# A decoder layer's feed-forward stage on one core: VectorE's list reordered, and two small computations moved to ScalarE

## The chip, the cores and the metric

The kernel runs on one core of a Trainium2 chip. The metric is device time in microseconds (us) from start to end of one execution. A core has five engines that each work through a list of their own, in order: TensorE (PE in the profile, its weight loads PEld), VectorE (DVE), ScalarE (ACT), GpSimd (POOL) and SyncE (SP, which here only starts DMAs). They are kept in step by semaphores alone: an instruction waits until a semaphore has reached a value, and what stands behind it in its engine's list waits too.

## The reference, cut to what matters

The program computes one decoder layer for 2048 tokens (4 sequences of 512) of width 512: attention with a sliding window, a layer in which each token goes through one of four experts, and a quantized gated feed-forward. Only the last is touched by the change. For a token row x (normalized without weights):

```
def activation_quant(x):                       # 8 bits, one scale per token
    s = 127 / clip(max(abs(x)), 1e-5)
    return clip(round(x * s), -128, 127) / s
def weight_quant(w):                           # -1, 0 or 1, one scale per matrix
    s = 1 / clip(mean(abs(w)), 1e-5)
    return clip(round(w * s), -1, 1) / s
h = silu(bit_linear(x, w_gate)) * bit_linear(x, w_up)     # 512 -> 2048
h = ln_weight * h * rsqrt(mean(h * h) + 1e-6)
y = bit_linear(h, w_down)                                 # 2048 -> 512
x = x + y
```

So the down product is one of small integers, multiplied at the end by a factor per token: the largest of the token's |h * ln_weight * rsqrt(...)| / 127 times the mean of |w_down|. In the kernel this factor is `y_scale`.

## The kernel before, in words

The feed-forward (`ffn_phase`, from L1580) goes over 16 tiles of 128 tokens, one token per partition. The 2048 h values of a token are made in FC = 4 chunks of 512 columns, called h value 0 to 3 here (the change calls them first to fourth). The work of a tile is spread over several rounds of the loops; every engine has one loop `for t in range(TILES)`, and in round t it does this:

- TensorE (`tensor_program`, L1881; `gate_up`, L1649): for each chunk c four matmuls for the gate and four for the up product of tile t, 512 columns each, and after each chunk a quarter of the down product of an earlier tile (LATE_DOWN = 2: two tiles back). The products go to two pairs of PSUM tiles in turn, so `gate_up(t, c)` waits until h value c - 2 has been formed (counted over the tiles too: `gate_up(t, 0)` waits for h value 2 of tile t - 1, `gate_up(t, 1)` for h value 3 of it, L1654). In the profile the gate tiles are `e_xT_ps` (even c) and `e_z_ps` (odd c), the up tiles `up_ps` and `e_aT_ps`.
- ScalarE (`scalar_program`, L1728): `gate_of(t, c)` (L1746) is the Silu of the gate product; `squares` (L1754) sums the squares of one half of h, 1024 columns; `pack` (L1739) turns the quantized half into bf16. The list of a round is: squares(t-1, 1), gate 0, normalize x of tile t+2, gate 1, turn-over of x's transpose, gate 2, pack(t-1, 0), pack(t-1, 1), gate 3, squares(t, 0).
- VectorE (`vector_program`, L1779): `hidden(t, c)` (L1784) forms h value c out of the up product and the gate. `top_of(t-1, n)` (L1800) is the largest of a half of the weighted h of the tile before, `sum_squares` (L1805 and L1807) forms its mean square plus epsilon, `scale_h` (L1813 to L1822) forms the factors, among them `y_scale` (L1819), `quantize_h` (L1831) multiplies and rounds both halves, and `y_of` (L1836) adds a finished down product to x. The rest is the normalization and quantization of x for tiles t+2 and t+3 (`front...`).
- GpSimd (`gpsimd_program`, L1681): h_rms as the power -0.5 of h_var (L1691), the weighting `weighted(t, c)` of each h value by `ln_w` into `xg_own` (L1695), two small operations for x, and the indirect DMAs that store a finished tile and gather a new one. In round t its list is: h_rms of t-1, weighted 0, 1, 2, rstd for x, weighted 3, gu_scale, store, gather.
- SyncE: the DMA transposes of the packed h (all tiles but the last, which TensorE transposes).

Each list is written out by hand; nothing plans it. Before the loop the experts' stage also forms the means of the three quantized weights, `w_mean`, and their reciprocals `w_scale` (L1462 and L1464), which ScalarE waits for before it quantizes the weights (L1380).

Of the kernel before, what the change touches and what calls it, by code (L numbers as in the profile page):

```python
# [54 lines left out]
CODE, CODE_ZERO = ROUND + 0x6600, 1536.0  # L55
XQ_STEPS, HQ_STEPS = 3, 5
LATE_DOWN = 2
# [1163 lines left out]
def expert_phase(nc, ctx, scratch, io, x1, x2, sh, front):  # L1221
# [7 lines left out]
    def sb(name, shape, dt=F32):  # L1229
        return ctx.enter_context(nc.sbuf_tensor(name, shape, dt))  # L1230
# [16 lines left out]
    abs_sum, abs_row, w_scale = sh["abs_sum"], sb("abs_row", [P, 3]), sb("w_scale", [P, 3])  # L1247
    plus_round = sb("plus_round", [P, 1])
    e_ones = sb("e_ones", [P, P])
    bn_st, bn_mv = sb("e_bn_st", [P, 2, 6]), sb("e_bn_mv", [P, 2, 2])  # L1250
# [118 lines left out]
    def scalar_program(act):  # L1369
# [6 lines left out]
        def shift(n):  # L1376
            c = stage_of(n)
            w = n // WCHUNKS
            act.wait_ge(w_loaded[c], n // STAGES * 16 + 16)
            act.wait_ge(scales_ready, 1)  # L1380
            nc.scalar.activation(w_stage[:, c, :], w_stage[:, c, :], ACT.Identity, scale=w_scale[:, w:w + 1], bias=plus_round[:])\
                .then_inc(w_shifted, 1)
# [27 lines left out]
    def vector_program(dve):  # L1410
# [51 lines left out]
        nc.vector.tensor_scalar(w_mean[:], sum_ps[:], 1.0 / (D * F), Q_EPS, ALU.mult, ALU.max).then_inc(mean_ready, 1)  # L1462
        dve.wait_ge(mean_ready, 1)
        nc.vector.reciprocal(w_scale[:], w_mean[:]).then_inc(scales_ready, 1)  # L1464
        dve.wait_ge(scales_ready, 1)

# [113 lines left out]
def ffn_phase(nc, ctx, io, x2, y, sh, front):  # L1580
# [31 lines left out]
    hw_max = sb("hw_max", [P, 2, 2])  # L1612
    h_ss, h_var, h_rms = sb("h_ss", [P, 1]), sb("h_var", [P, 1]), sb("h_rms", [P, 1])
    h_top, h_max, h_inv, h_mul = sb("h_top", [P, 1]), sb("h_max", [P, 1]), sb("h_inv", [P, 1]), sb("h_mul", [P, 1])
    y_scale = sb("y_scale", [P, LATE_DOWN + 2])

# [12 lines left out]
    hw_last_ready = sem("hw_last_ready")  # L1629
    ss_ready, h_var_ready, rms_ready = sem("ss_ready"), sem("h_var_ready"), sem("rms_ready")  # L1630
    hq_step, hq_ready = sem("hq_step"), sem("hq_ready")
# [96 lines left out]
    def scalar_program(act):  # L1728
# [12 lines left out]
        def gate_of(t, c):  # L1741
            act.wait_ge(gate_summed, t * FC + c + 1)
            act.wait_ge(gu_ready, t + 1)
            if c >= 2 or inside(t - 1):
                act.wait_ge(h_ready, t * FC + c - 1)
            nc.scalar.activation(gate[:, c % 2, :], gate_ps[c % 2][:], ACT.Silu, scale=gu_scale[:, t % 2, 0:1])\  # L1746
                .then_inc(gate_ready, 1)

        def squares(t, n):
            i = t % 2  # L1750
            act.wait_ge(h_ready, t * FC + 2 * n + 2)
            if n or inside(t - 1):
                act.wait_ge(sq_ready, t * HALVES + n)
            nc.scalar.activation(sq_junk[:], flat(h, i)[:, n * HALF:n * HALF + HALF], ACT.Square,  # L1754
                                 accum_out=h_sq[:, i, n:n + 1]).then_inc(sq_ready, 1)

        for t in range(TILES):
# [14 lines left out]
            if t == TILES - 1:  # L1772
                pack(t - 1, 1)
            squares(t, 0)
        squares(TILES - 1, 1)
        for g in range(FC):
            hqT_of(TILES - 1, g)

    def vector_program(dve):  # L1779
# [23 lines left out]
        def sum_squares(t):  # L1803
            dve.wait_ge(sq_ready, (t + 1) * HALVES)
            nc.vector.tensor_reduce(h_ss[:], h_sq[:, t % 2, :], AX.X, ALU.add).then_inc(ss_ready, 1)  # L1805
            dve.wait_ge(ss_ready, t + 1)
            nc.vector.tensor_scalar(h_var[:], h_ss[:], 1.0 / F, RMS_EPS, ALU.mult, ALU.add).then_inc(h_var_ready, 1)  # L1807

        def scale_h(t):
            i = t % 2  # L1810
            at = t * HQ_STEPS
            dve.wait_ge(hw_max_ready, (t + 1) * HALVES)
            nc.vector.tensor_reduce(h_top[:], hw_max[:, i, :], AX.X, ALU.max).then_inc(hq_step, 1)  # L1813
            dve.wait_ge(hq_step, at + 1)
            dve.wait_ge(rms_ready, t + 1)
            nc.vector.tensor_scalar(h_max[:], h_top[:], h_rms[:], Q_EPS, ALU.mult, ALU.max).then_inc(hq_step, 1)
            dve.wait_ge(hq_step, at + 2)
            nc.vector.reciprocal(h_inv[:], h_max[:]).then_inc(hq_step, 1)
            nc.vector.tensor_scalar(y_scale[:, t % (LATE_DOWN + 2):t % (LATE_DOWN + 2) + 1], h_max[:], w_mean[:, 2:3], 1.0 / QMAX, ALU.mult, ALU.mult)\  # L1819
                .then_inc(hq_step, 1)  # L1820
            dve.wait_ge(hq_step, at + 4)
            nc.vector.tensor_scalar(h_mul[:], h_inv[:], h_rms[:], QMAX, ALU.mult, ALU.mult).then_inc(hq_step, 1)  # L1822
# [11 lines left out]
        def y_of(t):  # L1834
            dve.wait_ge(y_summed, t + 1)
            nc.vector.scalar_tensor_tensor(xt[t], sums_of(t), y_scale[:, t % (LATE_DOWN + 2):t % (LATE_DOWN + 2) + 1], xt[t],  # L1836
                                           ALU.mult, ALU.add).then_inc(y_ready, 1)

        for t in range(TILES):
# [4 lines left out]
            if inside(t - LATE_DOWN - 1):  # L1844
                y_of(t - LATE_DOWN - 1)
            if inside(t - 1):
                top_of(t - 1, 1)
            hidden(t, 0)
# [3 lines left out]
            if inside(t - 1):  # L1852
                sum_squares(t - 1)
            if inside(t + 2):
                front.top_of_x(dve, t + 2)
# [3 lines left out]
            if inside(t - 1):  # L1859
                scale_h(t - 1)  # L1860
                quantize_h(t - 1)
            hidden(t, 2)
            if inside(t + 2):
# [162 lines left out]
```

## Time and profile before

| | |
|---|---|
| median of 3 runs | 789.06 us (788.45 to 791.21) |
| the profiled execution | 788.65 us, of which the trace's span is 786.6 us |
| TensorE busy | 734.1 us, 93% |
| VectorE busy | 592.7 us, 75% |
| ScalarE busy | 473.0 us, 60% |
| GpSimd busy | 331.8 us, 42% |
| mean granted TensorE clock | 0.989 |

The feed-forward's loop takes the part of the span from about 591 us to its end. In it the busy shares differ from the table: in the 40 slices of the profile, TensorE and VectorE both show 9 tenths or nearly there, ScalarE 6 to 7. Start times are counted from the first instruction; "busy" excludes semaphore waits; the name in a row's brackets is what an idle engine was released by. Successive instructions of one engine can overlap by some hundredths of a microsecond, so for the length of a list the distances from start to start count.

### The profile page before, as it was taken

The numbers are of one execution on the slowest core, as the hardware profiler recorded it, in microseconds if no ns is written. First come the engines' busy times: TensorE is split into PE (matmuls) and PEld (weight loads), VectorE is DVE, ScalarE is ACT, GpSimd is POOL, SyncE is SP. The second block draws the span as 40 slices with busy tenths as digits, with TensorE's granted clock in tenths as the row PEclk, the third lists the DMA queues.
The fourth block names the chain that finished last, engine by engine and source line by source line (L and its number), as shares of the span: only waits on it lengthen the run. The fifth ranks groups of instructions, "written<-read, shape, count | busy, mean of one in ns | idle before, by whom it ended". The sixth has DMA issues, their size and how long they took to land.

```text
span 786.6 us, 14189 instructions
## 1 busy us (share of the span) xinstructions
PE 734.1 (93%) x5167; PEld 509.8 (65%) x5184; DVE 592.7 (75%) x1099; ACT 473.0 (60%) x1028; POOL 331.8 (42%) x329
## 2 busy tenths in 40 slices
PE   5988999999999999999987989999998999999993
PEld 4765777777777776777764678888874444444441
DVE  6886866886667866766666547888888999999992
ACT  4565666766676665766666314444456777667761
POOL 2011205213242134254554444445546577778661
PEclk9999999999999999999999999999999999999998
DMA  9300012304030321314301366555341133334241
GB/s 311 119 1 27 28 47 89 105 31 162 29 108 28 108 93 70 108 38 152 129 34 55 54 216 261 186 200 196 118 134 30 41 95 80 98 91 107 70 92 40
DMA packets 55474, 78.33 MB, mean 100 GB/s; under 512 B 36335, under 2 KB 38383, under 8 KB 53680
## 3 DMA queue, kind: packets, MB, share of 16 engines
q1 hardware_dynamic: 46336, 51.99, 20.8%
q0 software_dynamic: 8784, 24.93, 9.7%
q8 instruction: 43, 0.70, 0.4%
q10 hardware_dynamic: 288, 0.52, 0.2%
q14 instruction: 23, 0.19, 0.1%
HBM read 56.92 MB, written 17.59 MB: 95 GB/s over the span
## 4 chain that ended last, share of the span: by engine, by line
PE 61%; DVE 21%; issue 7%; ACT 5%; POOL 3%; DMA 1%; another core or an unknown queue 0%; SPq 0%; ACTq 0%; POOLq 0%; DVEq 0%
PE side_ps L889 17%; PE pT_ps L976 9%; PE e_z_ps L1528 7%; PE y_ps L1528 7%; PE s_ps L948 5%; PE pv_ps L998 5%; DVE h L1784 4%; DVE hw_max L1800 4%; DVE hq_big L1831 3%; ACT hq L1739 2%; DVE neg_max L724 2%; PE s_ps L956 2%; PE pT_ps L889 1%; DVE probs L745 1%; ACT probs L548 1%
## 5 line engine op out<-in xcount | busy, mean ns | idle before, releaser
L548 ACT ACTIVATE probs<-s_ps,neg_max 128x512 f32<-128x512 f32 (+2 forms) x256 | 152.3, 610 | 18.6 <-DVE neg_max L724 17.1
L724 DVE TENSOR_REDUCE neg_max<-s_ps 128x2 f32<-128x1024 f32 (+2 forms) x128 | 124.5, 1014 | 36.2 <-PE s_ps L956 35.1
L976 PE MATMUL pT_ps<-ident,probs 128*128 128x128 f32 x832 | 115.7, 281 | 8.7 <-DVE probs L745 8.0
L560 ACT ACTIVATE probs<-pT_ps 128x512 f32<-128x512 f32 x96 | 57.4, 598 | 97.0 <-PE pT_ps L976 96.2
L976 PEld LDWEIGHTS pT_ps<-ident,probs 128*128 128x128 f32 x832 | 94.3, 144 | 23.9 <-DVE probs L745 10.6
L745 DVE COPY probs<-pT_ps 128x512 f32<-128x512 f32 x112 | 76.7, 685 | 38.9 <-PE pT_ps L976 35.9
L1695 POOL TENSOR_TENSOR xg_own<-h,ln_w_sb 128x512 f32<-128x512 f32 x63 | 82.8, 1324 | 33.2 <-DVE h L1784 33.1
L889 PE MATMUL side_ps<-w_hi 128*128 128x512 f32 x172 | 71.0, 413 | 0.0
L412 POOL TENSOR_TENSOR aT_hi<-norm,one_col 128x512 fp32r<-128x512 f32 x15 | 15.6, 1042 | 124.6 <-DVE norm L736 86.3
L889 PE MATMUL side_ps<-w_hi,w_lo 128*128 128x512 f32 x172 | 67.4, 392 | 0.0
L889 PE MATMUL side_ps<-w_lo,w_hi 128*128 128x512 f32 x172 | 67.0, 390 | 0.0
L1906 PE MATMUL y_ps<-w_tern,hqT 128*128 128x512 bf16 x210 | 54.5, 379 | 0.7
L998 PE MATMUL pv_ps<-probs,v_sb 128*32 128x256 f32 (+1 forms) x896 | 52.4, 368 | 1.9 <-DVE probs L745 0.9
L404 POOL TENSOR_TENSOR norm<-rinv,one_col 128x512 f32<-128x512 f32 x16 | 16.7, 1041 | 86.8 <-DVE rinv L731 86.8
L548 ACT ACTIVATION_READ_ACCUMULATOR probs<-s_ps,neg_max 128x1 f32 x256 | 52.9, 207 | 0.0
L1739 ACT ACTIVATE hq<-hq_big,minus_offset 128x1024 bf16<-128x1024 f16 x30 | 33.0, 1142 | 30.4 <-DVE hq_big L1831 30.4
L1657 PE MATMUL e_xT_ps<-w_tern,xqT_home 128*128 128x512 bf16 x126 | 32.7, 380 | 7.1 <-DVE h L1784 6.2
L1800 DVE TENSOR_REDUCE hw_max<-xg_own 128x1 f32<-128x1024 f32 x32 | 38.7, 1209 | 0.3
L998 PEld LDWEIGHTS pv_ps<-probs,v_sb 128*32 128x32 f32 x896 | 25.0, 109 | 19.6 <-issue 6.7
L889 PEld LDWEIGHTS side_ps<-w_hi,w_lo 128*128 128x128 f32 x172 | 32.3, 188 | 7.4
L1906 PEld LDWEIGHTS y_ps<-w_tern,hqT 128*128 128x128 bf16 x224 | 21.4, 98 | 23.3
L889 PEld LDWEIGHTS side_ps<-w_hi 128*128 128x128 f32 x172 | 32.4, 188 | 5.8 <-DVE k_lo L648 0.5
(290 smaller groups left out, 1782.8 us busy)
## 6 DMA issues: line engine op xcount, KB each, us to landing
w_piece<-w_ffn SPq DMA_DIRECT2D x24, 512.0 KB
w_stage<-w_ffn SPq DMA_DIRECT2D x12, 1024.0 KB
xres<-x POOLq DMA_DIRECT2D x4, 1024.0 KB, 6.4
xn<-x SPq DMA_DIRECT2D x3, 1024.0 KB
x<-xres POOLq DMA_DIRECT2D x3, 1024.0 KB, 4.8
xn<-c SPq DMA_DIRECT2D x2, 1024.0 KB, 5.0
v_next<-c SPq DMA_DIRECT2D x2, 1024.0 KB, 7.3
xn<-x SPq DMA_DIRECT2D x4, 256.0 KB, 3.7
```

Source lines behind the costliest of these rows:

```text
L548: nc.scalar.activation(weights[qt][:, h, at:at + width(qt)], s_ps[:, h, 0:width(qt)], ACT.Exp, bias=neg_max[:, qt % 2, h:h + 1], accum_out ...
L560: nc.scalar.activation(out, turned_p, ACT.Identity).then_inc(slot_copied[0], 1)
L724: nc.vector.tensor_reduce(neg_max[:, qt % 2, 2 * s:2 * s + 2], s_ps[:, 2 * s:2 * s + 2, 0:width(qt)], AX.X, ALU.max, negate=True).then_inc ...
L745: nc.vector.tensor_copy(weights[qt][:, :, a:z], pT_ps[:, 1, :].rearrange("p (h n) -> p h n", h=GH))\
L889: last = nc.tensor.matmul(out, lt, r, start=(first and n == 0), stop=(final and n == len(terms) - 1))
L976: last = nc.tensor.transpose(pT_ps[:, k % 2, h * P:h * P + P], weights[qt][:, h, a:z], ident[:])
L998: last = nc.tensor.matmul(pv_ps[HD * h:HD * h + HD, to], v_sb[:, slot, f:f + HD], p, start=first, stop=final, tile_position=(0, HD * h))
L1528: last = nc.tensor.matmul(out, lt[:, k, :], r[:, at, :], start=(n == 0), stop=(n == 3 * DK - 1))
L1695: nc.gpsimd.tensor_tensor(hw[:, t % 2, c, :], h[:, t % 2, c, :], ln_w[:, c * CHK:c * CHK + CHK], ALU.mult)\
L1739: nc.scalar.activation(hq[:, cols], hq_code[:, cols], ACT.Identity, bias=minus_offset[:]).then_inc(hq_packed, 1)
L1800: nc.vector.tensor_reduce(hw_max[:, i, n:n + 1], flat(hw, i)[:, n * HALF:n * HALF + HALF], AX.X, ALU.max, apply_absolute_value=True).then_ ...
L1906: last = nc.tensor.matmul(sums_of(t), hqT[:, t % 2, k, :], down_w[:, k, :], start=(k == 0), stop=(k == FK - 1))
```

## The change

VectorE's list in round t, before and after (what concerns x stays in place):

| before | after |
|---|---|
| mean of x, top 0, y_of | mean of x, top 0, y_of |
| **top 1**, h value 0, sum_squares | h value 0, sum_squares, **top 1** |
| top of x, h value 1, scale x, scale_h | top of x, h value 1, scale x, scale_h |
| **quantize_h**, h value 2 | h value 2, **quantize_h** |
| quantize x, statistics of x, h value 3 | quantize x, statistics of x, h value 3 |

sum_squares shrinks from two dependent instructions to one, since ScalarE now scales the values by 2048 ** -0.5 inside the Square activation. scale_h loses the forming of `y_scale`; ScalarE forms it with one activation on 128x1 values, at the end of round t for tile t - 1 (and for the last tile at the end), from `down_scale`, which VectorE forms once in the experts' stage.

```diff
-XQ_STEPS, HQ_STEPS = 3, 5
+XQ_STEPS, HQ_STEPS = 3, 4
...
+    down_scale = sh["down_scale"] = sb("down_scale", [P, 1])
...
-            act.wait_ge(scales_ready, 1)
+            act.wait_ge(scales_ready, 2)
...
+        nc.vector.tensor_scalar(down_scale[:], w_mean[:, 2:3], 1.0 / QMAX, None, ALU.mult).then_inc(scales_ready, 1)
         nc.vector.reciprocal(w_scale[:], w_mean[:]).then_inc(scales_ready, 1)
-        dve.wait_ge(scales_ready, 1)
+        dve.wait_ge(scales_ready, 2)
...
+        def y_scale_of(t):
+            n = t % (LATE_DOWN + 2)
+            act.wait_ge(hq_step, t * HQ_STEPS + 2)
+            if t >= LATE_DOWN + 2:
+                act.wait_ge(y_ready, t - LATE_DOWN - 1)
+            nc.scalar.activation(y_scale[:, n:n + 1], h_max[:], ACT.Identity, scale=down_scale[:]).then_inc(y_scale_ready, 1)
+
         def squares(t, n):
...
-            nc.scalar.activation(sq_junk[:], flat(h, i)[:, n * HALF:n * HALF + HALF], ACT.Square,
+            nc.scalar.activation(sq_junk[:], flat(h, i)[:, n * HALF:n * HALF + HALF], ACT.Square, scale=F ** -0.5,
...
             squares(t, 0)
+            if inside(t - 1):
+                y_scale_of(t - 1)
         squares(TILES - 1, 1)
+        y_scale_of(TILES - 1)
...
-            nc.vector.tensor_reduce(h_ss[:], h_sq[:, t % 2, :], AX.X, ALU.add).then_inc(ss_ready, 1)
-            dve.wait_ge(ss_ready, t + 1)
-            nc.vector.tensor_scalar(h_var[:], h_ss[:], 1.0 / F, RMS_EPS, ALU.mult, ALU.add).then_inc(h_var_ready, 1)
+            nc.vector.tensor_scalar(h_var[:], h_sq[:, t % 2, 0:1], h_sq[:, t % 2, 1:2], RMS_EPS, ALU.add, ALU.add)\
+                .then_inc(h_var_ready, 1)
...
+            if inside(t - 1):
+                dve.wait_ge(y_scale_ready, t)
             nc.vector.tensor_scalar(h_max[:], h_top[:], h_rms[:], Q_EPS, ALU.mult, ALU.max).then_inc(hq_step, 1)
...
-            nc.vector.tensor_scalar(y_scale[:, t % (LATE_DOWN + 2):t % (LATE_DOWN + 2) + 1], h_max[:], w_mean[:, 2:3], 1.0 / QMAX, ALU.mult, ALU.mult)\
-                .then_inc(hq_step, 1)
-            dve.wait_ge(hq_step, at + 4)
+            dve.wait_ge(hq_step, at + 3)
...
             dve.wait_ge(y_summed, t + 1)
+            dve.wait_ge(y_scale_ready, t + 1)
...
-            if inside(t - 1):
-                top_of(t - 1, 1)
             hidden(t, 0)
...
                 sum_squares(t - 1)
+                top_of(t - 1, 1)
...
                 scale_h(t - 1)
+            hidden(t, 2)
+            if inside(t - 1):
                 quantize_h(t - 1)
-            hidden(t, 2)
```

## Rows read from the trace of the kernel before

**Rows 1.** Windows, one round: us, busy us PE, PEld, DVE, ACT, POOL, clock, DMA.
```profile
653.34:664.58 11.24, 10.87 (x53) 4.76 (x53) 10.85 (x24) 8.07 (x13) 8.49 (x11) 1.00 0.34 93
```

**Rows 2.** Chain that ended last, same round: start us, us, what.
```profile
649.21 1.31 DVE hq_big L1831
...
653.34 0.75 DVE h L1784
```

**Rows 3.** Timeline of VectorE: start us, us, engine, line, operation, out<-in [idle before].
```profile
642.12 0.75 DVE L1784 SCALAR_TENSOR_TENSOR h<-e_aT_ps,gu_scale,f_gate 128x512 f32<-128x512 f32 x1
...
644.69 1.21 DVE L1800 TENSOR_REDUCE hw_max<-xg_own 128x1 f32<-128x1024 f32 x1
645.82 0.74 DVE L1784 SCALAR_TENSOR_TENSOR h<-up_ps,gu_scale,f_gate 128x512 f32<-128x512 f32 x1
646.48 0.14 DVE L1805 TENSOR_REDUCE h_ss<-h_sq 128x1 f32<-128x2 f32 x1
646.65 0.15 DVE L1807 TENSOR_SCALAR h_var<-h_ss 128x1 f32<-128x1 f32 x1
...
648.65 0.17 DVE L1818 RECIPROCAL h_inv<-h_max 128x1 f32<-128x1 f32 x1
648.73 0.20 DVE L1819 TENSOR_SCALAR y_scale<-h_max,w_mean 128x1 f32<-128x1 f32 x1
648.96 0.21 DVE L1822 TENSOR_SCALAR h_mul<-h_inv,h_rms 128x1 f32<-128x1 f32 x1
649.21 1.96 DVE L1831 TENSOR_SCALAR hq_big<-xg_own,h_mul 128x1024 f32<-128x1024 f32 x2
651.09 0.74 DVE L1784 SCALAR_TENSOR_TENSOR h<-up_ps,gu_scale,f_gate 128x512 f32<-128x512 f32 x1
...
653.08 0.15 DVE L1181 TENSOR_SCALAR f_var_eps<-f_bn_mv 128x1 f32<-128x1 f32 x1
```

**Rows 4.** Timeline of ScalarE, same round.
```profile
650.54 2.19 ACT L1739 ACTIVATE hq<-hq_big,minus_offset 128x1024 bf16<-128x1024 f16 x2 [2.17 <-DVE hq_big L1831]
652.64 0.67 ACT L1746 ACTIVATE f_gate<-e_z_ps,gu_scale 128x512 f32<-128x512 f32 x1
...
654.15 0.19 ACT L1754 ACTIVATION_READ_ACCUMULATOR sq_junk<-h 128x1 f32 x1
654.44 1.06 ACT L1754 ACTIVATE sq_junk<-h 128x1024 bf16<-128x1024 f32 x1
...
655.49 0.67 ACT L1746 ACTIVATE f_gate<-e_xT_ps,gu_scale 128x512 f32<-128x512 f32 x1
```

**Rows 5.** Groups of ScalarE by form: the smallest activation.
```profile
L525 ACT ACTIVATE k_hi<-side_ps,bk_sb 128x4 fp32r<-128x4 f32 x15 | 3.7, 245 | 0.0
```

**Rows 6.** Timeline of TensorE: the product that waits for h value 0.
```profile
646.61 1.04 PE L1657 MATMUL e_xT_ps<-w_tern,xqT_home 128*128 128x512 bf16 x4 [0.29 <-DVE h L1784]
```

**Rows 7.** Timeline of GpSimd, same round.
```profile
647.44 2.51 POOL L1695 TENSOR_TENSOR xg_own<-h,ln_w_sb 128x512 f32<-128x512 f32 x2
...
651.91 1.45 POOL L1695 TENSOR_TENSOR xg_own<-h,ln_w_sb 128x512 f32<-128x512 f32 x1 [1.96 <-DVE h L1784]
```

**Rows 8.** Timelines of the last tile but one: GpSimd, VectorE, ScalarE.
```profile
749.61 1.72 POOL L1695 TENSOR_TENSOR xg_own<-h,ln_w_sb 128x512 f32<-128x512 f32 x1
...
750.11 1.76 DVE L1831 TENSOR_SCALAR hq_big<-xg_own,h_mul 128x1024 f32<-128x1024 f32 x1
...
751.91 1.15 ACT L1739 ACTIVATE hq<-hq_big,minus_offset 128x1024 bf16<-128x1024 f16 x1 [0.53 <-DVE hq_big L1831]
...
753.67 0.75 DVE L1784 SCALAR_TENSOR_TENSOR h<-e_aT_ps,gu_scale,f_gate 128x512 f32<-128x512 f32 x1 [1.13 <-ACT f_gate L1746]
```

**Rows 9.** Timelines, the first and the last regular rounds: ScalarE, then VectorE.
```profile
600.10 0.67 ACT L1746 ACTIVATE f_gate<-e_xT_ps,gu_scale 128x512 f32<-128x512 f32 x1
...
609.00 0.75 DVE L1784 SCALAR_TENSOR_TENSOR h<-e_aT_ps,gu_scale,f_gate 128x512 f32<-128x512 f32 x1
...
743.17 0.75 DVE L1784 SCALAR_TENSOR_TENSOR h<-e_aT_ps,gu_scale,f_gate 128x512 f32<-128x512 f32 x1 [1.11 <-ACT f_gate L1746]
```

More of the change, by code:

```diff
@@ L1612, in ffn_phase @@
     hw_max = sb("hw_max", [P, 2, 2])
-    h_ss, h_var, h_rms = sb("h_ss", [P, 1]), sb("h_var", [P, 1]), sb("h_rms", [P, 1])
+    h_var, h_rms = sb("h_var", [P, 1]), sb("h_rms", [P, 1])
     h_top, h_max, h_inv, h_mul = sb("h_top", [P, 1]), sb("h_max", [P, 1]), sb("h_inv", [P, 1]), sb("h_mul", [P, 1])
-    y_scale = sb("y_scale", [P, LATE_DOWN + 2])
+    y_scale, down_scale = sb("y_scale", [P, LATE_DOWN + 2]), sh["down_scale"]
     hq_code = hq_big[:].bitcast(F16)[:, 0:2 * F:2]
@@ L1629, in ffn_phase @@
     hw_last_ready = sem("hw_last_ready")
-    ss_ready, h_var_ready, rms_ready = sem("ss_ready"), sem("h_var_ready"), sem("rms_ready")
+    h_var_ready, rms_ready, y_scale_ready = sem("h_var_ready"), sem("rms_ready"), sem("y_scale_ready")
     hq_step, hq_ready = sem("hq_step"), sem("hq_ready")
```

## The prediction

> **What bounds the kernel now.** I read the page's busy shares first, then the windows of a round, the chain of waits, and the timelines of the engines side by side. The loop runs in rounds of 11.22 us. In one, TensorE is busy 10.87 and VectorE 10.85 us [rows 1], so both look full, and TensorE once a round stands idle for 0.29 us until VectorE has formed h value 0 [rows 6]. That is the view in which moving h values forward looks right. The chain of waits shows something else: the round is closed by a ring that goes through ScalarE as well. It leads from the first half of quantize_h to h value 3 [rows 2] in 653.34 - 649.21 = 4.13 us, and what lies between is ScalarE's: pack 0 starts as the first half is written (650.54), pack 1 follows, and gate 3, which stands behind both in ScalarE's list, starts at 652.64 and ends at 653.31 [rows 4], 0.03 us ahead of h value 3. VectorE had started its last small instruction before that at 653.08 [rows 3]: it was ready a little before the gate, by some 0.2 us. So VectorE's list is the bound from h value 3 round to quantize_h, and ScalarE's from quantize_h to h value 3. A round is the sum of three legs:
>
> - h value 3 (642.12) to h value 0 (645.82): 3.70 us, VectorE's list [rows 3].
> - h value 0 to quantize_h (649.21): 3.39 us, VectorE's list [rows 3].
> - quantize_h to h value 3: 4.13 us, through ScalarE [rows 2, 4].
>
> Beside the first leg runs a second path, which is not yet late: gate 3, squares(t, 0), squares(t, 1), gate 0. Gate 0 starts 655.49 - 652.64 = 2.85 us after gate 3 and ends at 656.16 [rows 4]. Gate 3 starts 0.70 us ahead of h value 3, and h value 0 can start 0.03 us behind gate 0's end, so this path makes the leg at least -0.70 + 2.85 + 0.70 = 2.85 us. It has 0.85 us to spare.
>
> **The change part by part.**
>
> *Leg 1, h value 3 to h value 0.* top 1 leaves it: 645.82 - 644.69 = 1.13 us [rows 3]. VectorE's list would then need 3.70 - 1.13 = 2.57 us, but gate 0 is not there before 2.85. New on ScalarE, between squares(t, 0) and squares(t, 1), is the activation for y_scale. Before, squares(t, 1) started at 654.44, 0.10 after the accumulator read of squares(t, 0) had ended at 654.34 [rows 4]; that gap, about 0.1, takes part of the new instruction. Its price: no 128x1 activation is in the trace; the nearest is 128x4 at 0.245 us [rows 5], upper bound 0.67 - 0.10 = 0.57 (a 512-wide gate less the overlap with what follows it), lower bound 0, if it fits in the gap. I take 0.245 less about 0.1 of overlap with the next, less the part in the gap: 0.1. Its waits are met long before (h_max was written in the middle of the round, the y_of that frees the buffer two rounds ago). Leg 1: 2.95 us. So 0.75 is gained of the 1.13 taken out, and VectorE then idles some 0.4 us ahead of h value 0.
>
> By the Trainium skill (ScalarE: Activation LUTs, what an ACTIVATE costs), an activation with immediates takes 186 ns plus 0.833 ns per element, each per-partition pointer about 93 ns more, and successive ones overlap by about 93 ns. By that estimate the new one takes 0.19 us of the list; no run here shows it yet, and leg 1 would be 2.95 with it too.
>
> *Leg 2, h value 0 to quantize_h.* Added: top 1, 1.13, and h value 2, 646.48 - 645.82 = 0.66 [rows 3]. Gone: the sum of the squares, 646.65 - 646.48 = 0.17; y_scale, which stood between h_inv and h_mul: h_mul started 0.31 behind h_inv (648.65 to 648.96) and must now wait for h_inv itself, 0.17 and about 0.04 of semaphore (649.21 - 648.96 - 0.21), so 0.10 less; and quantize_h no longer starts right behind the h_mul that it needs: h value 2 needs nothing of it and can start 0.13 behind h_mul (0.21 less the 0.08 by which successive instructions overlap, as 645.82 + 0.74 and 646.48 show) where quantize_h needed 0.25, so 0.12 less. Leg 2: 3.39 + 1.13 + 0.66 - 0.17 - 0.10 - 0.12 = 4.79 us. No other wait is late in it: TensorE starts the product for h value 2 behind h value 0 [rows 6] and gate 2 is ready about 2.7 us after h value 0, h value 2 comes 4.1 after it. h_var is ready earlier in the list than before, and h_rms with it.
>
> *Leg 3, quantize_h to h value 3.* VectorE's list loses h value 2 here, 0.66, but the leg goes by ScalarE, so this gives nothing: VectorE waits longer for gate 3. What counts is when the two halves are written, and there GpSimd enters. The first half takes 1.31 us [rows 2], the second 1.96 - 1.22 = 0.74 [rows 3]. GpSimd's two weightings run from 647.44 to 649.95 [rows 7], and the first half ends 0.56 behind that: it waited 0.74 us for GpSimd. In the last round but one, a weighting issued at 749.61 took 1.72 us (1.28 in rows 7: 2.51 for two, with their overlap), and the second half, started at 750.11, took 1.76 [rows 8]: the two engines took turns, one whole instruction each. After the change h value 2 is formed before quantize_h, so its weighting is released 0.08 us behind it (651.83 to 651.91, [rows 3, 7]), right when the first half runs, and the second half must wait for it as in rows 8. Counted from h value 3: the weightings 0 and 1 end at 649.95 - 642.12 = 7.83 (their place behind GpSimd's store and gather does not depend on h value 0). quantize_h starts at 2.95 + 4.79 = 7.74, waits, and its first half is done at 8.39. By rows 8, pack 1 starts 751.91 - 749.64 = 2.27 us behind the end of the weighting (which ends some 0.03 behind the next one's issue at 749.61), and h value 3 comes 753.67 - 751.91 = 1.76 later. That makes the round 7.83 + 2.27 + 1.76 = 11.86 us, and leg 3 4.12, as long as before for another reason: the first half is quicker, the second slower.
>
> The rule for this stands in the Trainium skill (SBUF — State Buffer, "Who interferes with whom"): VectorE's tensor_scalar in a two-port mode and any GpSimd instruction hold a shared pair of ports exclusively, and who issues first goes first. The trace agrees (0.74 us of wait, and the 1.76).
>
> *Sum.* A round goes from 11.22 to 11.86 us. h value 3 of the first such round is at 609.00, of the thirteenth at 743.17 [rows 9]: 12 rounds in 134.2 us (the first two are shorter, since there is no y_of yet; after the change they are not, as y_of lies in the slack of leg 1). After: 12 x 11.86 = 142.3, +8.1 us. First round: gate 0 ends at 600.77 [rows 9], so h value 0 at 600.80, quantize_h at 605.59, h value 3 at about 609.8: +0.8. The rest, two rounds without work on x and the close: leg 2 and leg 1 trade as above (+0.5), the last h value 3 no longer stands behind the second half's wait (-0.2): +0.3. The new down_scale in the experts' stage is one 128x1 instruction of 0.15, once; the Square's scale costs nothing, being an operand of an instruction that is there. Sum +9.2 us on the profiled execution's 788.65 (span 786.6 and 2.05 around it), 797.9. That execution is 0.4 below the median of the runs shown, so I predict 798.0.
>
> What the numbers hang on: the legs' sum. A tenth of a microsecond in a round is 1.2 us in all. Likeliest case's own range 795 to 801: leg 1 between 2.85 and 3.1, leg 3 between 4.0 and 4.25.
>
> **The rivals.**
>
> *No net change.* The second half gets ahead of the weighting of h value 2. Then pack 0 starts 0.77 behind quantize_h (0.74 and 0.03), the packs take 2.10 and gate 3 0.70 [rows 4]: leg 3 is 3.57 and the round 2.95 + 4.79 + 3.57 = 11.31. Twelve rounds give 135.7, +1.5, and the other terms about 0: 790.2. For it: only 0.1 us separates quantize_h's start from GpSimd's end. Against: in rows 8 the weighting, issued while the first half held or awaited the ports, went ahead of the second half.
>
> *Faster.* The ring is looser than I read it, VectorE's own list is what counts, and TensorE gets its h values in time. VectorE's list shrinks by 0.17 + 0.10 + 0.12, and TensorE's 10.87 [rows 1] becomes the round: 12 x 0.36 = 4.3 us less than before, 784.3. For it: the 0.29 us idle of TensorE [rows 6]. Against: ScalarE runs its list in order, gate 3 is behind both packs and gate 0 behind both squares, and each ring leg is fixed by data.
>
> *Much slower.* The weighting of h value 2 goes ahead of the first half as well, from a start of quantize_h more than 0.1 us later than reckoned; each round then has another 1.2 us in it, some 812; or the y_scale activation costs 0.57, 11.86 + 0.35, some 802.
>
> **How the numbers follow.** Forecast 0.70, no net change 0.12, faster 0.12, much slower 0.06. 0.3% is 2.4 us, about what can be told from no change: 786.7 to 791.4 is the same. Faster 0.12 (its case), same 0.13 (its case and a little of the forecast's low tail), slower 0.75. The range for 8 in 10 reaches from the no-change case to the forecast's upper end: 789 to 801.
>
> **What would show it.** The changed profile should have rounds of 11.8 to 11.9 us; VectorE idle some 0.3 to 0.4 us before h value 0 and again before h value 3, both times until ScalarE's f_gate; quantize_h's second half at 1.7 us where the first was long before; TensorE idle about 1 us a round, ahead of gate_up(t, 1), which waits for h value 3, and VectorE's busy time down by about 0.3 us a round. Rounds of 11.3 with both halves short would mean the ports' order fell the other way; rounds of 10.9 that the ring through ScalarE was misread.

## The result: 803.42 us, 1.8% slower, and the profile after

The changed kernel takes 803.42 us (median of 4, 801.66 to 804.87) against 788.75 for the kernel before (787.71 to 791.21): ratio 1.0179, 95% interval 1.0159 to 1.0198. Slower was forecast, with 798.0 us; the time lies 2.4 us above the range's upper end of 801. The profiled execution took 801.66 us with a span of 799.9, 13.3 more than the span before.

The loop did nearly what the prediction's legs said. First the windows over one round, from h value 3 to the next (us; busy of PE, PEld, DVE, ACT, POOL; clock; DMA share; GB/s), to be set beside [rows 1]:

```profile
648.48:660.38 11.90, 10.71 (x51) 4.77 (x52) 11.11 (x23) 8.27 (x14) 8.80 (x10) 1.00 0.37 90
```

VectorE's timeline of the same round, beside [rows 3]:

```profile
648.48 0.75 DVE L1796 SCALAR_TENSOR_TENSOR h<-e_aT_ps,gu_scale,f_gate 128x512 f32<-128x512 f32 x1 [0.39 <-ACT f_gate L1748]
...
651.33 0.75 DVE L1796 SCALAR_TENSOR_TENSOR h<-up_ps,gu_scale,f_gate 128x512 f32<-128x512 f32 x1 [0.19 <-issue]
652.00 0.20 DVE L1817 TENSOR_SCALAR h_var<-h_sq 128x1 f32<-128x1 f32 x1
652.12 1.21 DVE L1812 TENSOR_REDUCE hw_max<-xg_own 128x1 f32<-128x1024 f32 x1
...
655.37 0.21 DVE L1833 TENSOR_SCALAR h_mul<-h_inv,h_rms 128x1 f32<-128x1 f32 x1
655.50 0.74 DVE L1796 SCALAR_TENSOR_TENSOR h<-up_ps,gu_scale,f_gate 128x512 f32<-128x512 f32 x1
656.16 0.75 DVE L1842 TENSOR_SCALAR hq_big<-xg_own,h_mul 128x1024 f32<-128x1024 f32 x1
656.82 1.76 DVE L1842 TENSOR_SCALAR hq_big<-xg_own,h_mul 128x1024 f32<-128x1024 f32 x1
...
660.38 0.75 DVE L1796 SCALAR_TENSOR_TENSOR h<-e_aT_ps,gu_scale,f_gate 128x512 f32<-128x512 f32 x1 [0.39 <-ACT f_gate L1748]
```

ScalarE's, beside [rows 4], with the packs apart and the new instruction between the two squares:

```profile
649.29 0.19 ACT L1763 ACTIVATION_READ_ACCUMULATOR sq_junk<-h 128x1 f32 x1
649.38 0.28 ACT L1756 ACTIVATE y_scale<-h_max,down_scale 128x1 f32<-128x1 f32 x1
649.57 1.06 ACT L1763 ACTIVATE sq_junk<-h 128x1024 bf16<-128x1024 f32 x1
...
656.94 1.15 ACT L1741 ACTIVATE hq<-hq_big,minus_offset 128x1024 bf16<-128x1024 f16 x1 [3.04 <-DVE hq_big L1842]
658.62 1.15 ACT L1741 ACTIVATE hq<-hq_big,minus_offset 128x1024 bf16<-128x1024 f16 x1 [0.53 <-DVE hq_big L1842]
659.67 0.67 ACT L1748 ACTIVATE f_gate<-e_z_ps,gu_scale 128x512 f32<-128x512 f32 x1
```

And GpSimd's weightings 1 and 2, and TensorE's product that waits for h value 3:

```profile
655.03 1.29 POOL L1697 TENSOR_TENSOR xg_own<-h,ln_w_sb 128x512 f32<-128x512 f32 x1
656.32 1.71 POOL L1697 TENSOR_TENSOR xg_own<-h,ln_w_sb 128x512 f32<-128x512 f32 x1
...
661.18 1.04 PE L1659 MATMUL e_z_ps<-w_tern,xqT_home 128*128 128x512 bf16 x4 [1.10 <-DVE h L1796]
```

These rows show the ring close: h value 2 ends at 656.24, weighting 2 follows at 656.32 and takes 1.71 instead of 1.28; the second half takes 1.76 where it took 0.74 [rows 3]; pack 1 waits 0.53 for it, gate 3 waits for pack 1, h value 3 waits 0.39 for gate 3, and TensorE waits 1.10 for h value 3.

Where the 13.3 us of span lie, by start times of the same instructions in both traces:

| stretch | before | after | more |
|---|---|---|---|
| start to the experts' first act_sb | 470.37 | 470.09 | -0.28 |
| experts' first to last act_sb | 115.55 | 117.11 | +1.56 |
| to the first h value 0 | 5.83 | 6.15 | +0.32 |
| to h value 3 of the first tile | 6.51 | 7.66 | +1.15 |
| to the next h value 3 | 10.74 | 11.59 | +0.85 |
| 12 rounds | 134.17 | 142.98 | +8.81 |
| to the last tile's quantize_h | 25.59 | 25.72 | +0.13 |
| from there to the end | 17.84 | 18.60 | +0.76 |

So 8.8 of the 13.3 us are the regular rounds, forecast as 8.1. The stretches ahead of the loop's second round, for which the prediction had nothing but 0.15 us, add 3.0. The first row of the table is left unexplained: over all the traces below, the start to the first act_sb varies from 466.66 to 471.57 us, so only distances behind it are compared between kernels.

### The profile page after: what moved, and what is told of

The parts are those of the page before. It is cut to its first block, busy times and chain, and to the rows that moved or that the text cites. A ratio compares the mean times of both kernels' runs of the same rounds, so it can differ in the third digit from the quotient of the medians.

```text
span 799.9 us, 14202 instructions
## 1 busy us (share of the span) xinstructions
PE 735.0 (92%) x5167; PEld 508.9 (64%) x5184; DVE 596.9 (75%) x1068; ACT 476.5 (60%) x1044; POOL 336.2 (42%) x329
## 4 chain that ended last, share of the span: by engine, by line
PE 60%; DVE 23%; issue 9%; ACT 3%; POOL 2%; DMA 1%; another core or an unknown queue 0%; DVEq 0%; ACTq 0%; POOLq 0%
PE side_ps L889 17%; PE pT_ps L976 9%; PE e_z_ps L1530 7%; PE y_ps L1530 7%; PE pv_ps L998 5%; PE s_ps L948 5%; DVE hq_big L1842 4%; DVE h L1796 3%; DVE hw_max L1812 3%; DVE neg_max L724 3%; PE s_ps L956 2%; DVE probs L745 2%; ACT f_gate L1748 1%; PE pT_ps L889 1%; PE pv_ps L990 1%
## 5 line engine op out<-in xcount | busy, mean ns | idle before, releaser
L976 PE MATMUL pT_ps<-ident,probs 128*128 128x128 f32 x832 | 114.0, 277 | 10.4 <-DVE probs L745 9.1
L976 PEld LDWEIGHTS pT_ps<-ident,probs 128*128 128x128 f32 x832 | 92.6, 142 | 25.6 <-DVE probs L745 11.9
L1697 POOL TENSOR_TENSOR xg_own<-h,ln_w_sb 128x512 f32<-128x512 f32 x63 | 86.1, 1375 | 19.0 <-DVE h L1796 18.5
L1659 PE MATMUL e_z_ps<-w_tern,xqT_home 128*128 128x512 bf16 x128 | 33.9, 388 | 16.8 <-DVE h L1796 16.8
L1842 DVE TENSOR_SCALAR hq_big<-xg_own,h_mul 128x1024 f32<-128x1024 f32 x32 | 37.8, 1224 | 0.0
```

Of the source, the lines that this page charges most:

```text
L976: last = nc.tensor.transpose(pT_ps[:, k % 2, h * P:h * P + P], weights[qt][:, h, a:z], ident[:])
L1697: nc.gpsimd.tensor_tensor(hw[:, t % 2, c, :], h[:, t % 2, c, :], ln_w[:, c * CHK:c * CHK + CHK], ALU.mult)\
L1842: nc.vector.tensor_scalar(hq_big[:, cols], flat(hw, i)[:, cols], h_mul[:], CODE, ALU.mult, ALU.add)\
```

## The experiments

The theory after the result, called A3 in the expectations: a round is a ring that goes through VectorE, GpSimd's weightings and ScalarE, and what costs is h value 2 ahead of quantize_h. Rivals: y_scale on ScalarE, or h value 0 forward. For the 3.0 us ahead of it: the new tile shifts the later ones. "Ports" stands for the shared pair of ports that the prediction names; what the traces show of it is that a quantization on VectorE and a weighting on GpSimd run one after the other, whole, and that the second of them takes longer than the 0.74 us (a half of quantize_h) or 1.28 us (a weighting) that it takes alone. All comparisons are with runs of the kernel before on the same chip. Where an edit says that addresses are as before, down_scale lies in `abs_row`, whose values are used up by then.

### The parts of the change apart

**e1_order.** VectorE's list as after, h_ss and y_scale as before:

```diff
-            if inside(t - 1):
-                top_of(t - 1, 1)
             hidden(t, 0)
...
                 sum_squares(t - 1)
+                top_of(t - 1, 1)
...
-                quantize_h(t - 1)
             hidden(t, 2)
+            if inside(t - 1):
+                quantize_h(t - 1)
```

> Only VectorE's list is reordered (h values 0 and 2 forward, as in the changed kernel); the sum of squares and y_scale stay on VectorE, no tile is added. Theory A (the round is a ring through ScalarE, and the reordering alone lengthens it): legs 2.85, 5.05 to 5.1 (h_ss and y_scale still in it) and 4.1 to 4.2, rounds of 12.0 to 12.1 us; the experts' stage as before (115.6 us from its first to its last act_sb), since no address moves; in all 10 to 12 us slower than before. Rival B (the reordering is harmless and the slowness comes from y_scale on ScalarE): rounds of 11.2 or below, time as before or less.

Measured: 801.77 against 786.59 us, ratio 1.0208 (1.0180 to 1.0236). Rounds of 12.14, leg 1 2.85, leg 2 5.07, leg 3 4.21 (645.62, 650.69 and 654.90 behind the h value 3 at 642.77), experts' stage 115.51. The legs are those expected; the loss, 15.2 us, is more than the 10 to 12 expected. The order alone makes the kernel slow, by a little more than the whole change does: with the small parts of the change the round is 11.90.

**e2_small.** The reverse: the order of before, the small parts of after, addresses as before (the edit is against the changed kernel):

```diff
-    down_scale = sh["down_scale"] = sb("down_scale", [P, 1])
+    sh["down_scale"] = abs_row
...
+            if inside(t - 1):
+                top_of(t - 1, 1)
             hidden(t, 0)
...
                 sum_squares(t - 1)
-                top_of(t - 1, 1)
...
                 scale_h(t - 1)
+                quantize_h(t - 1)
             hidden(t, 2)
-            if inside(t - 1):
-                quantize_h(t - 1)
```

> The order of before; only the small parts are changed (Square's scale, one instruction for h_var, y_scale on ScalarE), and down_scale lies in a tile that is free by then, so that no address moves. Theory A2 (also before, quantize_h's first half ended by GpSimd's weightings, which hold the ports, so its end does not depend on when it starts): leg 2 falls from 3.39 to 3.12, but the first half then takes 1.55 to 1.6 us instead of 1.3, the round stays at 11.2, time within 1 us of before. Rival (VectorE's list sets leg 2, as my prediction has it): rounds of 10.95, 3 us faster. If y_scale on ScalarE costs much: rounds over 11.3.

Measured: 786.46 against 786.59 us, ratio 1.0000 (0.9979 to 1.0021); rounds of 11.21 and, near both ends of the loop, 11.03 to 11.08 (11.16 to 11.21 before). quantize_h starts 6.86 us behind h value 3 (649.09 - 642.23) instead of 7.09 (649.21 - 642.12), and its first half takes that much longer:

```profile
649.09 1.52 DVE L1842 TENSOR_SCALAR hq_big<-xg_own,h_mul 128x1024 f32<-128x1024 f32 x1
```

1.52 against 1.31 [rows 2]. So already before the change the end of the first half was set by the end of GpSimd's weighting 1, and 0.2 us saved on VectorE bought nothing in these rounds. Their 11.22 was GpSimd's list as much as VectorE's. Over all 15 rounds the trace has 165.03 us instead of 165.89; what the small parts gain there they lose ahead of it, in the first tile (see e12_late_h0).

**e5_h0_only.** The changed kernel, addresses as before, with quantize_h back ahead of h value 2:

```diff
                 scale_h(t - 1)
-            hidden(t, 2)
-            if inside(t - 1):
                 quantize_h(t - 1)
+            hidden(t, 2)
```

> The changed kernel (addresses as before) with quantize_h back ahead of h value 2: only top 1 stands behind h value 0. Theory A3 (GpSimd's list is a part of the ring: weighting 1 ends 7.83 us behind h value 3 whatever VectorE does, and the first half cannot end sooner than 0.56 behind it): quantize_h starts at 7.1, its first half takes 1.3, h value 3 follows at 8.39 + 0.03 + 2.10 + 0.70 = 11.22: rounds of 11.2, time within 2 us of before. Rival (the h value 0 move is what costs, since gate 0 is late): rounds of 11.5 and more.

Measured: 787.24 against 788.76 us, ratio 0.9978 (0.9964 to 0.9993). Rounds of 11.22 where GpSimd has a gather in them, 10.83 where it has none; all 15 take 163.65 us. Moving h value 0 forward costs nothing. With the small parts it even makes the kernel faster, by 0.2%, a small gain whose interval is clear of no change.

**e6_h2_only.** The changed kernel, addresses as before, with top 1 back ahead of h value 0:

```diff
+            if inside(t - 1):
+                top_of(t - 1, 1)
             hidden(t, 0)
...
                 sum_squares(t - 1)
-                top_of(t - 1, 1)
```

> The changed kernel (addresses as before) with top 1 back ahead of h value 0: only h value 2 stands ahead of quantize_h. Theory A3: weighting 2 is released as quantize_h runs and goes between its halves; the weighting before it ends 7.83 behind h value 3, pack 1 starts 2.27 later, h value 3 1.76 after that: rounds of 11.86 to 11.9, as slow as the changed kernel (10 us over before), leg 1 3.70 again. Rival (the ring through VectorE and ScalarE alone, 3.70 + 3.66 + 4.2): 11.55. Rival (both moves are needed for the loss): 11.2.

Measured: 803.72 against 788.76 us, ratio 1.0185 (1.0158 to 1.0211). The whole loss is back, with h value 2's move alone. The rounds are not 11.9 but 12.45, which no expectation had. In those without a gather weighting 2 does go between the halves (0.81 and 1.76 us, at 628.94 and 629.67), and the round is 11.7 where it was 11.16 to 11.21 before. With a gather it goes another way. There, GpSimd's weightings 1 and 2, then quantize_h's first half:

```profile
651.49 1.28 POOL L1697 TENSOR_TENSOR xg_own<-h,ln_w_sb 128x512 f32<-128x512 f32 x1
652.71 1.27 POOL L1697 TENSOR_TENSOR xg_own<-h,ln_w_sb 128x512 f32<-128x512 f32 x1
...
652.32 2.23 DVE L1842 TENSOR_SCALAR hq_big<-xg_own,h_mul 128x1024 f32<-128x1024 f32 x1
```

Here the first half starts at 652.32, weighting 2 is issued 0.39 later, and goes first all the same: the half ends at 654.55, behind both. This is the prediction's "much slower" rival, in a neighbour of the kernel. So the kernel is as slow as the changed one, but in most rounds by another turn at the ports: that h value 2's move is enough for the loss is shown, not that it loses the same way.

### What stands ahead of the loop

**e3_places.** The changed kernel with nothing but down_scale moved into abs_row:

```diff
-    down_scale = sh["down_scale"] = sb("down_scale", [P, 1])
+    sh["down_scale"] = abs_row
...
-    h_var, h_rms = sb("h_var", [P, 1]), sb("h_rms", [P, 1])
+    h_ss, h_var, h_rms = sb("h_ss", [P, 1]), sb("h_var", [P, 1]), sb("h_rms", [P, 1])
```

> The changed kernel whole, but down_scale in a tile that is free by then and h_ss still allocated, so that every tile has the address of before. Theory (the 4 bytes shift the experts' operands, and their products then go at 233 instead of 229 ns): the experts' stage takes 115.6 us again instead of 117.1, the kernel is 1.5 us faster than the changed one, some 801 to 802 as a median; rounds still 11.9. Rival (the stage's pace is another thing, of the run or of the program's length): 117.1 here too.

Measured: 798.89 against 786.59 us, ratio 1.0174 (1.0142 to 1.0206). Its interval overlaps that of the changed kernel, so the times don't show the gain; the trace does: the experts' stage takes 115.50 us, rounds 11.90 (the second 12.20).

**e4_pad** and **e10_pad64.** The kernel before with one unused tile in that place, of 4 and of 64 bytes per partition:

```diff
     plus_round = sb("plus_round", [P, 1])
+    spare = sb("spare", [P, 1])        # e10_pad64: [P, 16]
     e_ones = sb("e_ones", [P, P])
```

> The kernel before with one unused 128x1 tile of 4 bytes allocated where the change puts down_scale; nothing else. If the shift of 4 bytes is what slows the experts' products: experts' stage 117.1 us instead of 115.6, in all 1.5 us slower than before, rounds unchanged at 11.2. If it is not: 115.6 and the time of before.

> The kernel before with an unused tile of 64 bytes per partition, in the place where 4 bytes made the experts' stage slower. If what counts is how the experts' operands lie within some unit of up to 64 bytes: 115.5 us for the stage, as without a tile. If any shift of the later tiles does it: 117.1.

Measured: e4_pad 788.49 against 786.59 us, ratio 1.0023 (1.0009 to 1.0038); e10_pad64 one run of 788.13, from which only the trace's stage is read. The windows from the first to the last act_sb, of the kernel before, with 4 bytes, with 64 bytes:

```profile
470.37:585.92 115.55, 114.83 (x575) 95.52 (x573) 92.81 (x172) 55.67 (x68) 54.48 (x57) 1.00 0.51 182
```

```profile
470.56:587.65 117.09, 116.41 (x574) 95.41 (x573) 92.84 (x171) 55.71 (x68) 54.46 (x57) 1.00 0.51 179
```

```profile
470.77:585.51 114.74, 114.06 (x575) 95.58 (x574) 92.81 (x172) 55.68 (x68) 54.41 (x57) 1.00 0.51 183
```

The stage's length follows where its tiles lie: 115.55, 117.09, 114.74 us at the same clock. Only PE's busy time moves with it: the mean of the experts' products at L1528 (y_ps from w_hi and e_aT_hi) is 391, 395 and 389 ns. The 1.56 us of the changed kernel are shown to be the unlucky 4 bytes of down_scale. Why 64 bytes are better than none stays open.

**e12_late_h0.** The kernel before, with some dead work ahead of the very first h value 0:

```diff
+    sh["abs_row"] = abs_row
...
+            if t == 0:
+                for n in range(3):
+                    nc.vector.memset(sh["abs_row"][:, n:n + 1], 0.0)
             hidden(t, 0)
```

> The kernel before with three 128x1 memsets of dead values on VectorE ahead of the very first h value 0, some 0.3 us. In the changed kernel that value came 0.3 us later, and then the quantization of x (L1206) in the first round took 1.85 instead of 0.47 us. Theory: the port's order turns on that delay, so h value 3 of the first tile comes 7.2 to 7.7 us behind h value 0 of it instead of 6.5. Rival (the loss comes from another part of the change): 6.5 here.

Measured: one run, 789.34 us; from the first h value 0 to h value 3 7.68 us, as in the changed kernel (7.66) and not as before (6.51). VectorE's timeline, the same quantization of x that the changed kernel has at 1.85:

```profile
595.26 0.75 DVE L1785 SCALAR_TENSOR_TENSOR h<-up_ps,gu_scale,f_gate 128x512 f32<-128x512 f32 x1 [0.71 <-PE up_ps L1658]
595.93 2.06 DVE L1206 TENSOR_SCALAR xq_big<-f_xn,x_inv 128x512 f32<-128x512 f32 x1
```

The delay is 0.42 us here (6.25 us from the last act_sb to the first h value 0, where it was 5.83 before and 6.15 in the changed kernel). So the +1.15 us is a turn at the ports, decided by a delay of 0.3 to 0.4 us. It belongs to the small parts of the change: the seven kernels that have them take 6.14 to 6.15 us to the first h value 0 and 7.66 to 7.68 from there, e2_small with the order of before and e3_places with the addresses of before among them; the other kernels, e12_late_h0 apart, take 5.81 to 5.84 and 6.50 to 6.60, e1_order and e4_pad among them. Ahead of the first h value 0 these parts add one VectorE instruction, the one that forms down_scale. What makes the first h value 0 late with it is not settled: the trace gives "issue" (0.24 us), and a like gap of 0.25 appears here, between two of the memsets; both kernels have another number of VectorE instructions ahead of that point.

### Taking the ring apart

**e7_gate3.** The changed kernel, addresses as before, with gate 3 ahead of both packs:

```diff
             gate_of(t, 2)
+            gate_of(t, 3)
             if inside(t - 1):
                 pack(t - 1, 0)
-            if inside(t - 1) and t < TILES - 1:
-                pack(t - 1, 1)
-            gate_of(t, 3)
-            if t == TILES - 1:
                 pack(t - 1, 1)
```

> The changed kernel (addresses as before), and in ScalarE's list gate 3 stands ahead of both packs (ScalarE idles there until quantize_h). Theory A3: h value 3 no longer waits for the packs; the ports' turns stay: the second half ends at 10.06 and h value 3 follows VectorE's own list at 11.4 behind the last: rounds of 11.35 to 11.45, 5 to 6 us faster than the changed kernel, and still 2 to 4 us slower than before. If only ScalarE's list were the limit: 10.8. If gate 3's place does not matter: 11.9.

Measured: 793.93 against 788.76 us, ratio 1.0070 (1.0043 to 1.0096), rounds of 11.40, as expected; the time is 5.2 us over before, where 2 to 4 were expected. Of the round's loss of 0.68 us, gate 3's place behind the packs was 0.50. In the 0.18 that is left, both halves still take their turns at the ports (0.81 and 1.76 us, at 651.32 and 652.04). Against before, the kernel also has the first tile's loss and 2.35 us more from the last tile's quantize_h to the end (20.19 against 17.84), which was not looked into.

**e8_both_lists.** The same, and GpSimd's store and gather between weightings 1 and 2:

```diff
             weighted(t, 1)
+            if inside(t - LATE_DOWN - 1):
+                store(t - LATE_DOWN - 1)
+            if t >= LATE_DOWN + 2 and inside(t - LATE_DOWN - 2 + len(homes)):
+                front.gather(pool, t - LATE_DOWN - 2 + len(homes))
             weighted(t, 2)
```

> As the kernel with gate 3 ahead of the packs, and in GpSimd's list the store and the gather stand between weighting 1 and weighting 2 (while quantize_h runs), where they stood ahead of h_rms. Theory A3: weighting 1 ends before quantize_h starts and weighting 2 begins after it: both halves take 0.75, the ring falls under TensorE's 10.8, rounds of 10.8 to 10.9, 13 us faster than the changed kernel and 3 to 5 us faster than before. Rival (the descriptors that GpSimd writes for the DMAs need the ports as well): halves of over 1 us, rounds of 11.2 and more.

Measured: 789.10 against 788.76 us, ratio 1.0012 (0.9994 to 1.0030). In the eight rounds that have both DMAs the mechanism works: one of 10.36 and seven of 10.94, both halves together

```profile
660.87 1.47 DVE L1839 TENSOR_SCALAR hq_big<-xg_own,h_mul 128x1024 f32<-128x1024 f32 x2
```

1.47 us. What it wins there, it gives back in rounds with the store alone (two of 11.75 and 12.32, the two halves 2.84), in the first tile (7.68 us instead of 6.51), in the two rounds behind it (11.12 and 11.32 instead of 10.74 and 10.75) and from the last h value 3 to the end (24.98 us instead of 22.45). The time forecast for it (3 to 5 us faster than before) was wrong by some 4 us for that reason.

**e11_gate3_before.** The kernel before with that edit of ScalarE's list alone, for all rounds but the last:

```diff
             gate_of(t, 2)
+            if t < TILES - 1:
+                gate_of(t, 3)
...
-            gate_of(t, 3)
+            if t == TILES - 1:
+                gate_of(t, 3)
             if t == TILES - 1:
                 pack(t - 1, 1)
```

> The kernel before, with gate 3 ahead of the packs alone. Theory A3: GpSimd's weighting 1 still ends 7.83 behind h value 3, the first half 0.56 later, then VectorE's own list: rounds of 11.03 instead of 11.22, some 2 us faster than before. If the packs were no limit: 11.2.

Measured: 786.13 against 788.09 us, ratio 0.9969 (0.9956 to 0.9983): faster than both kernels, by 2 us, as expected. Rounds of 11.10 against 11.22 (11.03 expected); h value 3 no longer waits for anything of ScalarE's:

```profile
648.59 0.69 ACT L1746 ACTIVATE f_gate<-e_z_ps,gu_scale 128x512 f32<-128x512 f32 x1 [1.90 <-PE e_z_ps L1657]
649.18 2.18 ACT L1739 ACTIVATE hq<-hq_big,minus_offset 128x1024 bf16<-128x1024 f16 x2
...
651.37 0.15 DVE L1181 TENSOR_SCALAR f_var_eps<-f_bn_mv 128x1 f32<-128x1 f32 x1
651.45 0.75 DVE L1787 SCALAR_TENSOR_TENSOR h<-e_aT_ps,gu_scale,f_gate 128x512 f32<-128x512 f32 x1
```

**e9_best.** e11 with GpSimd's gather between weightings 0 and 1:

```diff
             weighted(t, 0)
+            if t >= LATE_DOWN + 2 and inside(t - LATE_DOWN - 2 + len(homes)):
+                front.gather(pool, t - LATE_DOWN - 2 + len(homes))
             weighted(t, 1)
```

> The kernel before, with VectorE's list untouched; gate 3 stands ahead of the packs in ScalarE's list (all rounds but the last), and GpSimd's gather stands between weighting 0 and weighting 1, so that it runs while quantize_h does. Theory A3: in the rounds that have a gather both halves are free of the ports (1.4 to 1.5 us for the two), h value 3 waits for nothing of ScalarE's and the round is TensorE's own 10.8 to 10.9 us instead of 11.22; the others 10.75 to 11.1; in all 3 to 4.5 us faster than before. Rival (the rounds are set by VectorE's list alone): no change.

Measured: 796.75 against 788.09 us, ratio 1.0113 (1.0088 to 1.0138), rounds of 12.0 to 12.6, most of 12.4, where GpSimd has a gather. The expectation (3 to 4.5 us faster) was wrong, and by the ports again. The gather, weighting 1, then both halves:

```profile
659.46 1.02 POOL L1145 DMA_INDIRECT xn<-x,dense_rows  x1 [0.17 <-issue]
660.52 1.28 POOL L1695 TENSOR_TENSOR xg_own<-h,ln_w_sb 128x512 f32<-128x512 f32 x1
...
659.80 3.23 DVE L1834 TENSOR_SCALAR hq_big<-xg_own,h_mul 128x1024 f32<-128x1024 f32 x2
```

quantize_h starts 0.34 us into the gather, and its first half ends only behind weighting 1: the pair takes 3.23 us. In the one round in which it started 0.07 us into the gather (647.78), the first half took 0.75 and the second 2.16 us, again until a weighting (issued at 648.77) was through.

The rival written for e8_both_lists (the DMAs' descriptors need the ports as well) is not needed for this. The traces of e8_both_lists have the same start behind a store, once with a weighting right behind it and once without one. The second half of quantize_h and GpSimd's next weighting, in a round with the store alone and in one with both DMAs:

```profile
627.90 2.18 DVE L1839 TENSOR_SCALAR hq_big<-xg_own,h_mul 128x1024 f32<-128x1024 f32 x1
628.25 1.28 POOL L1697 TENSOR_TENSOR xg_own<-h,ln_w_sb 128x512 f32<-128x512 f32 x1
...
661.53 0.81 DVE L1839 TENSOR_SCALAR hq_big<-xg_own,h_mul 128x1024 f32<-128x1024 f32 x1
...
663.20 1.31 POOL L1697 TENSOR_TENSOR xg_own<-h,ln_w_sb 128x512 f32<-128x512 f32 x1
```

Both halves start 0.72 to 0.73 us into a store (issued at 627.18 and 660.80). Where no weighting stands behind the store, the half takes 0.81 us; where one does, it goes first and the half takes 2.18. So the store holds nothing up, the weighting does. For the gather that comparison is missing: that it holds the ports itself is neither shown nor excluded.

## Why the prediction was right or wrong

- **The bound, a ring through ScalarE**: right, and incomplete. GpSimd's weightings were in it before the change already (e2_small's 1.52 us). The prediction had that place in its numbers for leg 3 (7.83 us behind h value 3) but not in its account of what bounds the kernel before.
- **Leg 1, 2.95 us**: 2.85 (648.48 to 651.33). The y_scale activation, which I put at 0.1 us, costs nothing: it takes 0.28 (649.38), but squares(t, 1) starts 0.28 behind the accumulator read of squares(t, 0), where it was 0.29 behind before [rows 4]. It fits whole into the gap.
- **Leg 2, 4.79 us**: 4.83 (651.33 to 656.16). **Leg 3, 4.12 us**: 4.22 (656.16 to 660.38). Round 11.86: 11.90, and once, behind the first, 12.08. Twelve rounds +8.1: +8.8.
- **First round +0.8**: +0.85. **The rest +0.3**: +0.9. The last 0.76 of it is in the close, where the down product of the last tile but one waits 2.54 us for the DMA transposes instead of 0.40; that was seen and not tested. The close is 18.60 us here and, in the two other kernels with this order of VectorE's list and ScalarE's as before, 17.98 (e3_places) and 19.25 (e1_order).
- **The failed step** is the sum's last term, "The new down_scale in the experts' stage is one 128x1 instruction of 0.15, once". Its price was not the instruction's 0.15 us but its 4 bytes: 1.56 us in the experts' stage, shown by e4_pad and e3_places. Beside it stands a term that the sum lacked, the first tile: 0.32 and 1.15 us, which all kernels with the small parts have and those without them have not. Together that is 3.0 us, more than the 2.4 by which the range was missed. The 9.2 forecast (8.1 + 0.8 + 0.3; the 0.15 was named and not even added), and 1.56 + 1.47 + 0.71 and 0.05 (rounds) + 0.59 (close) - 0.28 (start), make the 13.3 of the traces. The medians differ by 1.4 us more than the two traces' spans do, which is within the runs' spread of 3 us. The last step of the sum has a slip as well: 797.9 and 0.4 are 798.3, not 798.0. The likeliest case's upper end had no room for a cost outside the loop.
- **Which edit costs**: the prediction's legs charge both moves (h value 0's with 1.13 us in leg 2 for 0.75 in leg 1), though its ring of 7.83 + 2.27 + 1.76 us hangs on h value 2's alone. The experiments charge only h value 2's: e5_h0_only is not slower, e6_h2_only is as slow as the whole.
- **The signs**: the rounds, the second half (1.76) and TensorE's wait (1.10) came as named. VectorE's busy time was to fall by 0.3 us a round and rose from 10.85 to 11.11: time in which an instruction stands started and waits for the ports is counted as busy, and the two halves now take 2.51 us together instead of 2.05.
- **The order at the ports**: forecast to be weighting 2 between the halves, which it was (1.76 us). The Trainium skill's rule (SBUF — State Buffer, "Who interferes with whom"), that the one who issues first goes first, agrees with that but not with e6_h2_only, going by the start times of the traces: there quantize_h had been waiting for 0.39 us when weighting 2 was issued, and weighting 2 went first. Nor does it agree with the rounds of e8_both_lists that have the store alone (627.90 and 628.25), or with the first tile of the changed kernel (L1206 started at 598.22, the weighting at 598.51). In [rows 8] a VectorE instruction in the same position went first. What decides between an instruction that waits and one that stands right behind the running one in the other engine's list stays open.

## What to carry to other kernels

Follow the chain once round the loop and through every engine before moving an instruction forward: what an early result releases elsewhere (here a weighting that takes the ports from the next step of the critical chain) can cost more than the wait that it ends. If an engine waits for a gate that stands in its maker's list behind something later, reorder that list: this was the edit that gained most over the kernel before, 2.0 us (e5_h0_only gained 1.5). A new small tile is not free where matmuls read tiles allocated behind it; put it last or into dead space, and compare the untouched stages of both traces first. One small instruction is not free either where it shifts the start of a stage: the first tile took 1.5 us more with it.

## What the runs showed of the hardware

- The pace of the experts' products hangs on where their tiles lie: the stage took 115.55 us, 117.09 with 4 bytes ahead and 114.74 with 64, all at clock 1.00.
- VectorE's quantization and GpSimd's weighting take turns in whole instructions: 0.74 and 1.28 us alone became 1.76 and 1.71 (656.82 and 656.32), and a VectorE instruction can stand behind two weightings in a row (2.23 us at 652.32 in e6_h2_only).
- A weighting right behind another GpSimd instruction can go ahead of a VectorE instruction that started 0.3 to 0.7 us before it (2.18 us instead of 0.81 in e8_both_lists, 2.57 instead of 0.75 in e9_best). A store with no weighting behind it did not hold VectorE's quantization up (0.81).
- A 128x1 activation whose scale is read from a 128x1 tile takes 0.28 us, and here took nothing of the list, since it fitted between the accumulator read and the next activation (starts 0.28 us apart with it, 0.29 without).
